# Four stages of a graph transformer in one block: barriers removed, neighbouring turns interleaved, weights loaded ahead

## What is computed

```python
x = x + _L0_gnn_ref(_layernorm(x), adj, ...)   # masked attention, 4 heads, then a layer norm with gamma and beta
x = x + _L0_ffn_ref(_layernorm(x), ...)        # 8 experts, the best 2 of each token, gelu
x = x + _L1_gnn_ref(_layernorm(x), adj, ...)   # masked attention, 8 heads
x = x + _L1_ffn_ref(_layernorm(x), ...)        # 30 steps of: h += 0.01*tanh(h); h *= sigmoid(h); layer norm; h = h @ W.T + b
```

## Time and profile before

| what | value |
|---|---|
| median of 3 runs | 2860.79 us (2860.59 to 2861.35) |
| the profiled execution | 2858.99 us |
| its span in the profile | 2857.1 us |
| mean granted TensorE clock | 0.987 |
| a0, from the start to its last instruction on POOL | 0 to 415.98 us |
| m | 416.45 to 926.93 us |
| a1 | 927.20 to 1532.46 us |
| d | 1532.93 us to the end |

### The profile page before, as it was taken

The page is one execution under the profiler, slowest core; times in us unless marked ns, Lnnn a source line. Parts: engine busy times, 40 slices in busy tenths (PEclk is TensorE's granted clock), DMA queues, the critical chain, the costliest instruction groups (busy, mean ns, idle before and its releaser), DMA issues. The chain is left out here.

```text
span 2857.1 us, 69846 instructions
## 1 busy us (share of the span) xinstructions
PE 2727.0 (95%) x20703; PEld 1796.3 (63%) x20703; DVE 2522.4 (88%) x6982; ACT 2125.5 (74%) x4032; POOL 1741.4 (61%) x1152
## 2 busy tenths in 40 slices
PE   6999959999999799999996999999999999999999
PEld 3666638888888466666665555555555555555556
DVE  4999968888888577777777999999999999999999
ACT  4777734444444566666665999999999999999994
POOL 2667653333332233333321999999999988888882
PEclk9999989999999899999998999999999999999999
DMA  5000000000000000000000555555555555555555
GB/s 151 23 26 22 22 16 1 0 0 0 0 0 1 27 16 15 15 15 15 16 8 27 188 204 203 191 199 205 192 196 207 192 193 206 197 192 203 204 188 171
DMA packets 132585, 281.78 MB, mean 99 GB/s; under 512 B 11760, under 2 KB 69152, under 8 KB 132512
## 3 DMA queue, kind: packets, MB, share of 16 engines
q1 hardware_dynamic: 115616, 272.44, 27.7%
q10 hardware_dynamic: 16896, 8.39, 1.0%
HBM read 270.49 MB, written 10.29 MB: 98 GB/s over the span
## 5 line engine op out<-in xcount | busy, mean ns | idle before, releaser
L1368 POOL TENSOR_TENSOR xn_sb<-xn_sb,d_rb 128x1024 f32<-128x1024 f32 x464 | 1084.2, 2372 | 153.3 <-DMA d_rb<-d_rstd_rows 153.1
L1521 PE MATMUL d_p_y<-xn_sb,d_w_main 128*128 128x512 f32 x1856 | 952.6, 595 | 0.0
L1535 PEld LDWEIGHTS d_p_gt<-ident,xn_sb 128*128 128x128 f32 x3840 | 438.9, 140 | 559.5 <-ACT xn_sb L1575 416.8
L1400 DVE BATCH_NORM_STATS2 d_stats<-d_p_gt 128x6 f32<-128x256 f32 x1920 | 718.6, 413 | 0.0
L1575 ACT ACTIVATE xn_sb<-d_th,d_bias 128x512 f32<-128x512 f32 x928 | 666.8, 719 | 11.7 <-DVE d_th L1393 0.9
L1393 DVE SCALAR_TENSOR_TENSOR d_th<-d_th,d_p_y 128x512 f32<-128x512 f32 x960 | 640.6, 667 | 4.1 <-ACT d_th L1571 3.9
L1571 ACT ACTIVATE d_th<-d_p_y,d_bias 128x512 f32<-128x512 f32 x928 | 625.5, 674 | 0.0
L1535 PE MATMUL d_p_gt<-ident,xn_sb 128*128 128x128 f32 x3840 | 583.7, 275 | 9.8 <-DVE d_stats L1400 8.6
L1103 DVE SCALAR_TENSOR_TENSOR x_sb<-m_p_y,m_combine,x_sb 128x128 f32 (+1 forms) x1024 | 311.4, 343 | 68.8 <-PE m_p_y L1145 52.2
L1192 ACT ACTIVATE m_hidden<-m_p_h,m_cols 128x512 f32<-128x512 f32 x256 | 176.5, 689 | 225.9 <-PE m_p_h L1137 225.9
L371 DVE TENSOR_REDUCE a_row_max<-a_p_s 128x4 f32<-128x512 f32 x384 | 238.1, 682 | 88.1 <-PE a_p_s L509 87.9
(11 more groups left out here) (210 smaller groups left out, 3921.7 us busy)
## 6 DMA issues: line engine op xcount, KB each, us to landing
d_rb<-d_rstd_rows SPq DMA_DIRECT2D x464, 512.0 KB, 5.5
a_adj_in<-in_adj_dram SPq DMA_DIRECT2D x64, 256.0 KB, 2.9
out_dram<-d_out_sb ACTq DMA_DIRECT2D x32, 256.0 KB, 2.6
d_rstd_rows<-d_rstd_row SPq DMA_DIRECT2D x116, 16.0 KB, 1.4
m_w_sb<-in_L_ffn_w_dram SPq DMA_DIRECT2D x2, 512.0 KB
x_sb<-in_x_dram SPq DMA_DIRECT2D x1, 256.0 KB, 2.8
a_w_raw<-in_L_gnn_Wq_dram SPq DMA_DIRECT2D x2, 64.0 KB, 2.1
a_w_raw<-in_L_gnn_Wk_dram SPq DMA_DIRECT2D x2, 64.0 KB, 2.1
```

The lines of the kernel that those rows point to most:

```text
L1368: nc.gpsimd.tensor_tensor(g[:, c, :], g[:, c, :], rb[:, buf, :], ALU.mult).then_inc(s_gs, 1)
L1400: ins = nc.vector.bn_stats(stats[:, q % 2, (j * CT + t) // 2].rearrange("p a s -> p (a s)"), p_gt[:, t * P:(t + 2) * P].rearrange("p (a c) ...
L1521: nc.tensor.matmul(p_y[:, c % 2, cols(u)], w_main[:], g[:, c, cols(u)], start=True, stop=True).then_inc(s_y, 1)
L1535: ins = nc.tensor.transpose(p_gt[:, t * P:(t + 1) * P], g[:, c, t * P:(t + 1) * P], ident[:])
```

## The change

All four stages are now generators inside one `nc.Block()`. Each has a program for each engine that yields at certain turns, and `turns` calls them in one order that is the same on every engine. Semaphores take the place of the barriers: `after` hands a stage the counters of the one before. Constants are made at the head of POOL's program. SBUF is given out from two ends ("left" for the attentions, `rb` and `out_sb`; "right" for m, `xn_sb` and the rest of d), so that neighbours don't overlap; tiles of a1 lie where those of a0 lay. PSUM banks are shared by neighbours, hence the waits of PE on `context` and `projected`.

```diff
+        def turns(a0, m, a1, d):
+            for program in (a0, m, a0, a0, a0, a0, m, a0, m, a0, a0, m, a0, m, a0, m, m, a1, d, m, a1, a1, m,
+                            a1, a1, a1, a1, a1, d, a1, a1, d):
+                next(program, None)
...
+        with nc.Block() as block:
+            @block.sync
+            def _(sp):
+                turns(a0.sync(sp), m.sync(sp), a1.sync(sp), d.sync(sp))
```

```diff
 def quads(eng, body):
-            for j in (-1, 0, 1):
-                body(2 * j, 0)
-                body(2 * j + 1, 1)
+        for k in (-2, -1):
+            body(k, k % 2)
+            yield
+        for k in range(4):
+            body(k, k % 2)
...
+        for k in range(QUADS - 4, QUADS + 2):
+            body(k, k % 2)
+            if k > QUADS - 4:
+                yield
```

```diff
+            for w, source in ((w_q, Wq), (w_k, Wk), (w_v, Wv), (w_o, Wo)):
+                sp.dma_start(w[:], source).then_inc(s_w, 16)
...
+            if isinstance(k, int) and k == -1:
+                take_weights()
+                dve.wait_ge(s_fill, n_fill)
             if live(k):
                 maxima(k)
                 take_maxima(k, p_w)
+            if isinstance(k, int) and k == 0:
+                split_bias()
...
+    def tensor(pe):          # a1, in b-1
+            pe.wait_ge(after["added"], after["all"])
+    def scalar(act):         # a1, in b-1
+                nc.scalar.activation(warm[:], minus_half[:, 0:1], ACT.Exp)
```

The experts and the recurrent stage wait for the quads that they read, and ACT runs one activation of the function that comes next ahead of its first use:

```diff
 def mixture_ffn(...):
+            if isinstance(k, int) and live(k + 2, GROUPS):          # DVE
+                dve.wait_ge(after["updated"], k + 3)
+            elif not isinstance(k, int):
+                dve.wait_ge(after["updated"], after["quads"])
...
+            if isinstance(k, int) and k == 0:                       # PE
+                pe.wait_ge(after["context"], after["quads"])
+                pe.wait_ge(after["projected"], after["quads"])
...
+                nc.scalar.activation(warm[:], minus_half[:, 0:1], ACT.Gelu)   # ACT, k == -1
 def recurrent_ffn(...):
+            pe.wait_ge(after["normed"], 2 * c + 2)                  # PE, transpose_x
+            if c >= 2:
+                pe.wait_ge(after["projected"], after["quads"])
...
+        yield
+        nc.scalar.activation(warm[:], env["minus_half"][:, 0:1], ACT.Tanh)
                 act.wait_ge(s_prep, 1)
-                iterations(act, body)
+        yield from iterations(act, body)
```

More of the change, by code:

```diff
@@ new lines, in graph_attention @@
+    p_s = pb("p_s", [P, 4, QG, P])
+    p_w = pb("p_w", [P, QUAD])
+    p_z = pb("p_z", [P, QUAD])
+    p_x = pb("p_x", [P, QUAD])
+    p_y = pb("p_y", [P, QUAD])
+    s_w = sem("weights_loaded")
+    s_wb = sem("biases_loaded")
+    if normed:
+        s_wt = sem("weight_transposed")
+    s_prep = sem("prep_chain")
+    s_fill = sem("fills")
+    pieces = [0, 1, 6, QUADS] if x_in is not None else [0]
+    s_x = [sem(f"x_loaded_{i}") for i in range(len(pieces) - 1)]
+    s_adj = [sem(f"adj_loaded_{i}") for i in range(2)]
@@ new lines, in mixture_ffn @@
+    same = sb("same", [P, GT, E])
+    place = sb("place", [P, GT, E])
+    first = sb("first", [P, GT, E])
+    second = sb("second", [P, GT, E])
+    top = sb("top", [P, 2, GT])
+    where = sb("where", [P, 2, GT])
+    gap = sb("gap", [P, GT])
+    ratio = sb("ratio", [P, GT])
+    total = sb("total", [P, GT])
+    ones = sb("ones", [P, GT])
+    minus_one = sb("minus_one", [P, GT])
+    weighted = sb("weighted", [P, 2, GT, E])
+    share = sb("share", [P, 2, GT])
+    combine = sb("combine", [P, 2, GT, E])
@@ new lines, in mixture_ffn, with live, wait, groups @@
+    s_b2a = sem("b2_added")
+    s_h = sem("hidden_product")
+    s_gelu = sem("hidden_ready")
+    s_y = sem("output_product")
+    s_acc = sem("output_added")
+    def live(q, limit):
+        return not isinstance(q, int) or 0 <= q < limit
+    def wait(eng, s, value):
+        if not isinstance(value, int) or value > 0:
+            eng.wait_ge(s, value)
+    def groups(eng, body):
+        for k in (-2, -1, 0, 1):
+            body(k, k % 2)
+            yield
+        with eng.Fori(1, GROUPS // 2 - 1) as j:
+            body(2 * j, 0)
+            body(2 * j + 1, 1)
+        yield
+        body(GROUPS - 2, 0)
+        yield
+        body(GROUPS - 1, 1)
@@ L1378, in _ @@
[L1378 to L1380 removed]
+                make_constants(nc, pool, env)
+                turns(a0.gpsimd(pool), m.gpsimd(pool), a1.gpsimd(pool), d.gpsimd(pool))
             @block.vector
             def _(dve):
[L1384 to L1389 removed]
@@ L1564, in _ @@
[L1564 removed]
+                turns(a0.tensor(pe), m.tensor(pe), a1.tensor(pe), d.tensor(pe))
             @block.scalar
             def _(act):
[L1568 to L1575 removed]
```

2780 lines of the change are left out of this document (1406 added, 1374 removed).

## The result

The changed kernel takes 2840.11 us in the median of 4 runs (2835.75 to 2842.61), against 2860.69 before. The ratio is 0.9927, with a 95% interval of 0.9915 to 0.9939. The gain is 20.6 us, where 35.2 were forecast, and the time lies 2 us above the range. The profiled execution took 2839.76 us, its span is 2838.0 (2857.1 before).

The account below looks back on a forecast made before the run. Inside stages one engine is nearly always full (PE or DVE); only at three boundaries do all fall idle. Shifts 2.1 + 18.4 + 6.3 + 8.4 = 35.2 us take the median from 2860.79 to 2825.6 us, range 2812 to 2838.

Parts of the forecast that it names:

- Start, 2.1: Kernel start: the load of adj_in for quad 2 lands at 41.2 instead of 43.3, gaining 2.1 us; bounds 0 and 6.
- From which the old rhythm runs on: Method at start and boundaries: time one instruction's new arrival and assume the turns behind it keep their old pace.
- some 9: Start: what the shorter preparation would be worth in us if the mask did not come last.
- First attention to experts, 18.4: First boundary: first expert add 19.0 us earlier, 20.2 with PE's slack, less 1.8 for slow PE; bounds 13 and 24.
- I take off two such losses, 1.8: First boundary: deduction for PE's slower products after standing idle some 5 us, 1.91 against 1.05 us per 8 products.
- the lower bound, 13: First boundary: gain if PE stays slow for a whole group of outputs and b34 costs its 3.4 us openly.
- Experts to second attention, 6.3: Middle boundary: the second attention's first maxima come at 941.8 instead of 948.06, gaining 6.3 us; bounds 2 and 10.5.
- The 8.2 us of DVE work: Middle boundary: second attention's tables, bias, statistics, deviation and xn, standing on DVE between b30 and b31 while PE waits.
- 1.5 more for a slow PE: Middle boundary: extra lateness of the experts' last add, on top of 6.2 us, putting it at 934.6.
- Second attention to recurrent stage, 8.4: Last boundary: first statistics start at 1531.2 instead of 1539.64, three of four table loads hidden, gaining 8.4 us; bounds 6 and 10.
- No change inside the stages: Within the stages: the change leaves the work as it is, so only the start and three boundaries shift; 0 us.
- the cold boundaries: Rival, chance 0.08: start and all three boundaries give only their lower bounds, 0 + 13 + 2 + 6 = 21, so 2840 us.

Follow-up runs that it names:

- experiment 7: Changed kernel with unread transposes put ahead of three PE waits, in the experts' groups 0, 1 and 31: 2830.84 us, ratio 0.9895.
- experiment 1: Changed kernel without interleaving, each stage's turns placed wholly behind those of the stage before: 2842.95 us, ratio 0.9936.
- experiment 4: Changed kernel with the second attention's preparation placed behind the experts' last group instead of before it: 2836.2 us, ratio 0.9913.
- experiment 5: Changed kernel with the experts' preparation placed behind the first attention's turn 31 instead of around turn 30: 2839.44 us, ratio 0.9930.
- experiment 6: Changed kernel with the second attention's DVE preparation cut into ten steps, each behind one expert's adds of groups 30 and 31: 2829.73 us, ratio 0.9890.
- experiment 2: Changed kernel with the adj loads for quads 2 and 3 issued ahead of the last piece of x: 2826.11 us, ratio 0.9875.
- experiment 3: Changed kernel with adj loads for quads 2 and 3 issued behind all of x but ahead of the experts' weights: 2834.41 us, ratio 0.9903.
- experiment 9: Changed kernel with experiments 2 and 6, unused transposes at groups 0, 1 and behind the last expert, experts' weights loaded before x's last piece, split behind turn 0: 2810.59 us.

## Why the prediction was wrong

**The step that failed** is the price of an idle PE: nothing at the start, 1.8 us at the first boundary and 1.5 at the middle one. With PE kept busy at the last two and all else unchanged (experiment 7) the kernel is 9.3 us faster, of the 14.5 that the forecast was off. The mechanisms at the boundaries were named with their places; three of the four terms were mis-sized, and the fourth came within 1.1 us.

- *Start, 2.1, measured -0.4.* The mask moved by 1.5 (forecast 2.1). "From which the old rhythm runs on" failed: the old rhythm has a PE that is busy at this point, the new one has a PE that has been idle for 10.34 us, and its next turn took 12.35 instead of 10.59. The other 0.5 went in the turns up to quad 29. This profile is a good one: in the five others with the same loads (experiments 1 and 4 to 7) the mask came at 41.80 to 43.80 and quad 29 0.4 to 2.9 us later than before. So the landing was at best 1.6 earlier, and the cost of the idle PE, put at nothing, took all of it. That the mask comes last was right, and experiment 2 gives what freeing it is worth: 11.1 us by the marks, where I had written "some 9".
- *First attention to experts, 18.4, measured 13.3.* The replay of the chain to the first add held within 0.8 us (421.65, less the 0.4 by which the turns ahead were late, against 420.4). The step behind it, "I take off two such losses, 1.8", failed: the loss was 4.6. Experiment 7, which keeps the clock up, gives 2.8 of it back. The rest, 1.8, is the turn of group 1, 17.18 us with a steady one at 15.37; it is as long with PE at full clock (17.19), and is the wait for b34's normalisation, 1.33 us for POOL and 1.12 of work. I had named both in the lower bound, 13, and not in the sum. The 1.2 us of slack that I added did not show.
- *Experts to second attention, 6.3, measured -0.5.* This is below my lower bound of 2. The 8.2 us of DVE work came as 8.3. But the last add was 11.7 late, where 6.2 + 1.5 = 7.7 was forecast (8.2 less two outputs of 1.05 is 6.1, not 6.2); then 8.6 us to the maxima, not 7.2; then a second turn of 9.04, not 7.70. "1.5 more for a slow PE" was worked out for one set of products, and PE ran at half clock through three of them and again in the first turn of the second attention. Experiment 7 gives 5.7 us for it. Experiment 4 shows that interleaving in this form was the mistake here: without it the boundary is 4.8 us shorter. Experiment 6 shows that it is the lump that costs: the same work in ten pieces gives 10.3. (Each of the three against the changed kernel's profile; the ranges stand behind the marks.)
- *Second attention to recurrent stage, 8.4, measured 7.3 to 7.8.* Right by its mechanism and nearly in size. (From 1528.7 the terms lead to 1531.1, not 1531.2.) The table load took 1.28 with no drain behind it, 0.01 us from its end to silu. The Trainium skill's 2.66 (ScalarE: Activation LUTs, What ACT_TABLE_LOAD costs) again finds no second half in this trace.
- *No change inside the stages*: right to 0.5 us. DVE's rows in the recurrent stage, which were to stay as they were, grew all the same (last section).

Of the rivals the cold boundaries came, with 0 + 13 + 2 + 6 = 21 against 20.6 measured. It had a chance of 0.08, and its own time, 2840, lay outside the range of 2812 to 2838, which I had said takes in most of it. That the sum fits so well is in part luck: the middle boundary came 2.5 below its bound, the last one 1.3 above. The signs for it were in the earlier trace rows and in the row of 1.91 against 1.05 in the earlier trace rows. I charged the clock for each set of products and not for the whole time until it rose again.

**What stays open.** The boundary costs differ between executions with the same instructions. Ahead of `m_p_xt` 31 five profiles of the same turns took 523.63 to 528.11. In experiment 4 the clock falls a second time, behind a wait of PE of 1.63 us that passes without a loss in the changed kernel's profile:

```profile
445.04 1.13 PE L1219 MATMUL m_p_y<-m_w_sb,m_hidden 128*128 128x128 f32 x8 [1.63 <-DVE x_sb L1183]
446.10 1.74 PE L1264 MATMUL m_p_b<-m_b_blocks,m_combine_t 32*128 32x512 f32 x2
...
449.22 1.91 PE L1219 MATMUL m_p_y<-m_w_sb,m_hidden 128*128 128x128 f32 x8
```

In the windows the clock is 1.00 from 436 to 445 and 0.50 from 447 to 453. That turn took 20.35 us, and 17.18 in the changed kernel. Experiments 2 and 3 have the second fall too (20.35 and 20.37), experiment 6 has not (17.16). So whether this short wait costs the clock makes 3.2 of the 4.5 us of spread at this boundary. The Trainium skill (TensorE: Matmul & The Clock Gate, What's actually happening) says that the chip's watch over PE's activity runs freely, not from the kernel's start, so the same kernel is met at another phase each time. The rows agree; no run here fixes the phase. So a single profile's term is good to some 4 us at this boundary and to 2 at the two others, my readings of before among them. Which of the five is typical was not settled.

## What to carry to other kernels

When stages are joined, ask of each piece that is put ahead of the old stage's tail which engine it holds up and for how long beyond the free buffers. An 8 us lump on DVE between two groups cost more than it hid; the same work in pieces of 0.4 to 1.1 us, each behind one product's add, cost 1.5 us and saved 7.0. Price an idle PE by the whole stretch until the clock is back, 3 to 6 us here for waits of 3.5 to 7, and not by the next instruction. Before shortening a preparation, look at what comes last: one load of 0.25 MB behind 6.8 MB was worth 11 us by the marks and 14 by the medians, and with that load in its old place the rewritten preparation gained nothing.

## What the runs showed of the hardware

- Transposes whose results nobody reads, put into three of PE's waits, made the kernel 9.3 us faster (2830.84 us instead of 2840.11).
- A wait of PE of 1.63 to 1.65 us, with PE busy ahead of it, was followed by a granted clock of 0.50 in three of five profiles of the same turns, and not in the two others.
- In the recurrent stage the records of DVE became 0.28 us longer in the changed kernel's profile (median of the mix 0.941 us, 0.665 before; of the statistics 0.685 and 0.410), while the pace of the stage stayed the same to 0.3 us in 1272. In the ten experiments, with the same instructions there, the median of the mix is 0.683 to 0.725. A mean duration by itself was no sign of a slower stage. Why the records grew was not settled.
- One issue in SP's queue took 25.97 us right behind the last piece of `x`, with 4 KB to move itself (SP's queue of the kernel after). In experiment 9, where only quads 1 to 5 stand ahead of it, it took 5.46:

```profile
7.63 25.97 SPq L1042 DMA_DIRECT2D m_rows_in<-in_L_ffn_router_w_dram  x1
```

- DVE's subtraction and POOL's additions on SBUF took longer side by side. The two rows of the kernel after overlap by 1.0 us, and POOL's addition of beta just ahead (371.32, 1.67 us) covers the rest of DVE's. Apart from each other DVE's takes 1.23 (experiment 9) and POOL's two 1.27 each:

```profile
371.89 2.18 DVE L1099 TENSOR_TENSOR m_w_lo<-m_w_sb,m_w_hi 128x1024 fp32r<-128x1024 f32 x1
```

```profile
373.07 2.14 POOL L318 TENSOR_TENSOR x_sb<-x_sb,a_proj_n 128x512 f32<-128x512 f32 x1
```
